# A pre-norm decoder layer: first normalisation split by batch, and the first projections reordered around it

## The reference

```python
x = x + attention(layernorm(x))          # 16 heads of 16, causal, Wq Wk Wv Wo with biases
x = x + cross_attention(layernorm(x), ctx, mask)   # 512 memory tokens, no weights
x = x + moe(layernorm(x))                # router, top 4 of 16 experts, gated FFN

def layernorm(x): return (x - mean(x)) / sqrt(var(x) + 1e-5)
Q = (X @ Wq.T + bq) * scale;  K = (X @ Wk.T + bk) * scale;  V = X @ Wv.T + bv
```

## Time and profile before

| | value |
|---|---|
| median of three runs | 232.58 us |
| the profiled execution's own time | 232.66 us |
| its span in the trace | 230.9 us |
| PE busy | 222.6 us, 96% |
| DVE busy | 179.4 us, 78% |
| ACT busy | 130.1 us, 56% |
| POOL busy | 75.2 us, 33% |

### The profile page before, as it was taken

How to read it: one execution, slowest core, us unless ns; L and a number is a source line. 1 busy time by engine, 2 the same in 40 slices (tenths; PEclk the granted TensorE clock), 3 DMA queues, 4 the chain that set the end, 5 groups by cost and what they waited for, 6 DMA issues and landing times.

```text
span 230.9 us, 4563 instructions
## 1 busy us (share of the span) xinstructions
PE 222.6 (96%) x1481; PEld 177.8 (77%) x1481; DVE 179.4 (78%) x431; ACT 130.1 (56%) x258; POOL 75.2 (33%) x65
## 2 busy tenths in 40 slices
PE   7999989998999999989999999999999999999995
PEld 2588767875485788778888888888888888888884
DVE  3779896969267458679889879879879879879775
ACT  2138999766341617384484384385385385375561
POOL 6621460001002010426426426425425435435222
PEclk9999999999999999999999999999999999999999
DMA  5991042000000000022422431331331330410002
GB/s 170 381 387 34 0 140 91 3 4 0 0 3 0 0 0 4 0 62 76 139 60 77 136 71 65 136 79 57 136 88 48 136 102 34 136 45 0 1 3 91
DMA packets 7856, 17.30 MB, mean 75 GB/s; under 512 B 913, under 2 KB 2978, under 8 KB 7714
## 3 DMA queue, kind: packets, MB, share of 16 engines
q1 hardware_dynamic: 7232, 16.52, 21.8%
q10 hardware_dynamic: 610, 0.60, 0.9%
HBM read 16.59 MB, written 0.52 MB: 74 GB/s over the span
## 4 chain that ended last, share of the span: by engine, by line
PE 79%; DVE 9%; ACT 6%; issue 3%; POOL 2%; POOLq 0%; DVEq 0%; ACTq 0%
PE PS L1119 34%; PE PS L1135 20%; PE PS L987 3%; ACT pr L382 3%; PE PS L1001 3%; PE PS L1085 3%; DVE masked L668 2%; PE PS L947 2%; PE PS L961 2%; PE PS L978 2%; PE PS L895 2%; PE PS L883 1%; DVE HL L798 1%; PE PS L1165 1%; DVE qpar L574 1%
## 5 line engine op out<-in xcount | busy, mean ns | idle before, releaser
L296 POOL TENSOR_TENSOR WLg<-raw_g,WHg 128x1024 fp32r<-128x1024 f32 x16 | 38.2, 2390 | 58.4 <-ACT WHg L352 58.4
L793 DVE SCALAR_TENSOR_TENSOR pt<-pt 128x512 f32<-128x512 f32 x30 | 49.4, 1646 | 4.2 <-DVE pt L789 2.2
L478 ACT ACTIVATE HH<-pt 128x512 fp32r<-128x512 f32 x30 | 18.9, 632 | 52.3 <-DVE pt L793 52.1
L1119 PE MATMUL PS<-XH,WHg 128*128 128x512 f32 x120 | 47.0, 392 | 0.0
L1119 PE MATMUL PS<-XL,WHg 128*128 128x512 f32 x120 | 46.9, 390 | 0.0
L1119 PE MATMUL PS<-XH,WLg 128*128 128x512 f32 x120 | 46.7, 389 | 0.0
L1135 PE MATMUL PS<-WHd,HH 128*128 128x256 f32 x120 | 35.3, 294 | 1.0 <-DVE HL L798 0.8
L1135 PE MATMUL PS<-WLd,HH 128*128 128x256 f32 x120 | 33.9, 282 | 0.0
L1135 PE MATMUL PS<-WHd,HL 128*128 128x256 f32 x120 | 33.9, 282 | 0.0
L303 POOL TENSOR_TENSOR WLd<-raw_w,WHd 128x512 fp32r<-128x512 f32 x16 | 20.7, 1296 | 32.9 <-ACT WHd L358 32.9
L798 DVE TENSOR_TENSOR HL<-pt,HH 128x512 fp32r<-128x512 f32 x30 | 22.2, 738 | 11.0 <-ACT HH L478 11.0
(11 more groups left out here) (154 smaller groups left out, 358.5 us busy)
## 6 DMA issues: line engine op xcount, KB each, us to landing
raw_g<-we_d SPq DMA_DIRECT2D x16, 512.0 KB, 4.0
raw_w<-we_d SPq DMA_DIRECT2D x16, 256.0 KB, 2.6
ctxT<-ctxT_d SPq DMA_DIRECT2D x1, 1024.0 KB, 10.1
ctx_sb<-ctx_d SPq DMA_DIRECT2D x1, 1024.0 KB, 12.3
wqkv<-wqkv_d SPq DMA_DIRECT2D x3, 256.0 KB, 6.1
out_d<-x SPq DMA_DIRECT2D x4, 128.0 KB, 1.7
rows<-rows_d ACTq DMA_DIRECT2D x1, 264.0 KB, 5.7
x<-x_d ACTq DMA_DIRECT2D x2, 128.0 KB, 2.8
```

The lines of the kernel that those rows point to most:

```text
L296: g.tensor_tensor(WLg[slot][:, :, :, :].rearrange("p k g f -> p (k g f)"), raw_g[slot][:, :], WHg[slot][:, :, :, :].rearrange("p k g f -> ...
L478: a.activation(HH[slot][:, m, :], hid[:, m, :], ACT.Copy).then_inc(hh_done, 1)
L793: v_.scalar_tensor_tensor(out=hid[:, m, :], in0=glu[:, m, :], scalar=GLU_MAX, in1=upc[:, m, :], op0=ALU.min, op1=ALU.mult).then_inc(hid_do ...
L1119: i = t.matmul(PS[:, 2 * m + part, :], w[slot][:, k, part, m * P:(m + 1) * P], xx[:, k, :], start=(n == 0), stop=(n == 3 * KD - 1))
```

## The change

The first normalisation is done for each batch by itself. On DVE: statistics of chunks 0 and 1 and their variances, then statistics of chunks 2 and 3, then xn of batch 0, variances of batch 1, xn of batch 1. POOL takes two powers over two columns in place of one over four, and sets the constant part of vp after them. PE turns batch 0, projects K and Q of the first half of the heads for batch 0, then turns batch 1, then projects K and Q for batch 1. ACT issues `rows` after `params` and the mask.

```diff
-            g.memset(vp[:, :, :, DH:HP], 1.0)
...
-                chunks = slice(0, NC) if n == 0 else slice((n - 1) % B * QC, (n - 1) % B * QC + QC)
+                chunks = slice(n % B * QC, n % B * QC + QC)
...
             rstds(0)
+            rstds(1)
+            g.memset(vp[:, :, :, DH:HP], 1.0)
...
-            act.dma_start(rows[:, :], rows_d.rearrange("(a n) -> a n", a=1).to_broadcast([P, 2 * D + E])).then_inc(row_in, 16)
             act.dma_start(params[:, :], params_d).then_inc(param_in, 16)
             act.dma_start(mask8[:, :], mask_d.rearrange("(a n) -> a n", a=1)).then_inc(mask_in, 16)
+            act.dma_start(rows[:, :], rows_d.rearrange("(a n) -> a n", a=1).to_broadcast([P, 2 * D + E])).then_inc(row_in, 16)
...
-            for c in range(NC):
-                dve.wait_ge(x_in[c], 16)
-                row_stats(x, c)
-            variances(0, range(NC))
-            normalise(x, 0, range(NC))
+            def first_stats(b):
+
+                for c in range(b * QC, (b + 1) * QC):
+                    dve.wait_ge(x_in[c], 16)
+                    row_stats(x, c)
+
+            first_stats(0)
+            variances(0, (0, 1))
+            first_stats(1)
+            normalise(x, 0, (0, 1))
+            variances(1, (2, 3))
+            normalise(x, 1, (2, 3))
...
-            for b in range(B):
-                transposes(xn, b, b, xn_done, (b + 1) * QC)
+            def project_half(j, m, bank, b):
+
+                pe.wait_ge(xT_done[b], 1)
+                for k in range(KD):
+                    i = t.matmul(PS[:, bank, b * S:(b + 1) * S], wqkv[:, j, k, m * P:(m + 1) * P], xT[:, k, b * S:(b + 1) * S],
+                                 start=(k == 0), stop=(k == KD - 1))
+                return i
...
+            transposes(xn, 0, 0, xn_done, QC)
             pe.wait_ge(qkv_in[1], 16)
-            project_heads(1, 0, 4, k_ps)
+            project_half(1, 0, 4, 0)
             pe.wait_ge(qkv_in[0], 16)
-            project_heads(0, 0, Q_BANK[0], q_ps)
+            project_half(0, 0, Q_BANK[0], 0)
+            transposes(xn, 1, 1, xn_done, NC)
+            project_half(1, 0, 4, 1).then_inc(k_ps, 1)
+            project_half(0, 0, Q_BANK[0], 1).then_inc(q_ps, 1)
             project_heads(1, 1, 5, k_ps)
```

More of the change, by code:

```diff
@@ L315, in _ @@
             low_gate_up(1, 1)
-            for n in range(1, 5):
+            for n in range(2, 6):
                 rstds(n)
@@ L540, in variances @@
             def variances(n, chunks):
-                dve.wait_ge(bn_done, NC if n == 0 else NC + n * QC)
+                dve.wait_ge(bn_done, (n + 1) * QC)
                 for c in chunks:
@@ L632, in context_scale @@
                 cs = slice(b * QC, (b + 1) * QC)
-                dve.wait_ge(rstd_done, b + 2)
+                dve.wait_ge(rstd_done, b + 3)
                 link(v_.tensor_scalar(xscale[:, cs], rstd[:, cs], D ** -0.5, None, ALU.mult))
@@ L725, in _ @@
             context_stats(1)
-            variances(3, (0, 1))
-            normalise(x3, 3, (0, 1))
+            variances(4, (0, 1))
+            normalise(x3, 4, (0, 1))
             context_max(2)
@@ L742, in _ @@
             context_stats(3)
-            variances(4, (2, 3))
-            normalise(x3, 4, (2, 3))
+            variances(5, (2, 3))
+            normalise(x3, 5, (2, 3))
             low_x(2, slice(S, S + P))
@@ L886, in _ @@
             pe.wait_ge(ident_done, 1)
-            for b in range(B):
-                transposes(xn, b, b, xn_done, (b + 1) * QC)
-            def project_heads(j, m, bank, done):
[L892 to L897, removed]
+            def project_half(j, m, bank, b):
[4 more added lines that the diff above has]
+                return i
+            def project_heads(j, m, bank, done):
+                project_half(j, m, bank, 0)
+                project_half(j, m, bank, 1).then_inc(done, 1)
+            transposes(xn, 0, 0, xn_done, QC)
             pe.wait_ge(qkv_in[1], 16)
-            project_heads(1, 0, 4, k_ps)
+            project_half(1, 0, 4, 0)
             pe.wait_ge(qkv_in[0], 16)
-            project_heads(0, 0, Q_BANK[0], q_ps)
+            project_half(0, 0, Q_BANK[0], 0)
+            transposes(xn, 1, 1, xn_done, NC)
+            project_half(1, 0, 4, 1).then_inc(k_ps, 1)
+            project_half(0, 0, Q_BANK[0], 1).then_inc(q_ps, 1)
             project_heads(1, 1, 5, k_ps)
```

## The result

The changed kernel takes 233.81 us (median of 16 runs, 233.07 to 235.06) against 232.80 us (16 runs, 232.44 to 234.33) for the kernel before: ratio 1.0036, 95% interval 1.0020 to 1.0052. It is slower, by 0.5 to 1.2 us; the prediction said 233.5, in a range of 232.6 to 234.2, and gave "slower" 0.80. The profiled execution has a span of 231.5 us, 0.6 more than before.

The account below looks back on a forecast made before the run. PE's completion of Q was taken to bound the kernel, shifting the end one for one: projections start 0.41 us earlier, but batch 1's transposes and copy lie bare, so 12.59 becomes 13.52, +0.93, giving 233.5 us, range 232.6 to 234.2.

Parts of the forecast that it names:

- The warm-up term: PE at the head: batch 0's transposes start when the 14 warm-ups end, 6.90; uncertain by up to +0.17 us.
- a sign of being wrong: DVE after the projections: queries starting before 13.1, against 13.5 expected, would show the forecast wrong.
- The weights term: Transfers of K's and Q's weights: Q's land at 8.3 for a use at 9.2, so zero.
- The rows' move: Transfer of rows, issued 1.0 us later: landing at 8.5, or 9.5 at the far end; taken as zero.
- The memset: POOL, vp's constant part, 0.94 us: may hold batch 1's xn to 9.3, but costs nothing by itself.
- The port: Rival, DVE against POOL: late rows let xb block bup and maskf, DVE is the end; +1.4, 234.0; chance 0.12.
- The clock: Rival, PE: longer gaps undo the clock's rise, half of 5 us lost; +0.93 + 2.5, 236.0; chance 0.04.
- Absorption of Q's shift: Rival, attention loop from 17 us on: it absorbs the shift; 0 to -0.2, 232.5; chance 0.12.
- The kept start: Rival, PE: gaps half as long, so the 0.41 us earlier start is kept; +0.3, 232.9; chance 0.08.

Follow-up runs that it names:

- e2: Kernel before with PE's new order alone; normalisation, memset and rows as before: ratio 1.0067 to the kernel before.
- e3: Changed kernel with batch 1's transposes between K and Q of batch 0: ratio 1.0003 to the kernel before.
- e9: e3 with vp's memset back ahead of the powers: ratio 0.9983 to the kernel before, median 232.38 us.
- e11: e1 (changed kernel, old order on PE) with vp's memset ahead of the powers: ratio 0.9987 to the kernel before.
- e1: Changed kernel with PE's old order put back; split normalisation, later memset and later rows stay: ratio 1.0021 to the kernel before.
- e6: Changed kernel with 12 warm-up matmuls instead of 14: ratio 1.0031 to the kernel before.
- e4: Changed kernel with rows issued ahead of params and the mask, as before: ratio 1.0064 to the kernel before.
- e5: Changed kernel with DVE's parity, bup and maskf ahead of its copy of xT: ratio 1.0040 to the kernel before.
- e10: Changed kernel with Q's weights issued on ACT's queue instead of SP's: ratio 1.0032 to the kernel before.
- e12: Changed kernel with five edits together, e9's two plus those of e5, e10 and e6: ratio 0.9992 to the kernel before.
- e7: Kernel before with 12 warm-up matmuls instead of 14: ratio 1.0008.
- e8: Kernel before with rows issued behind params and the mask, nothing else: ratio 0.9985.

## Why the prediction was right

| step | predicted | measured |
|---|---|---|
| transposes of batch 0, start | 6.90 | 6.34 |
| their copy on ACT | 7.60 | 7.05 |
| K of batch 0 | 8.36 | 7.79 |
| transposes of batch 1 | 10.04 | 9.69 |
| DVE's copy | 10.74 | 10.33 |
| PE's next load | 11.49 | 11.07 |
| Q complete | 13.52 | 13.08 |
| queries start | 13.5 | 13.11 |
| shift of the masked scores | +0.93 | +0.49 |
| time | +0.93 | +1.01 by medians, +0.84 by the ratio, 0.5 to 1.2 |

**What bounds.** Q's completion sets the end one for one: shown by the thirteen profiles of the table. The order on PE as the cause is shown from three sides: alone it costs 1.0 to 2.1 us (e2); with the transposes moved ahead by four records the loss is gone (e3, and clear of the noise with the memset early, e9); and put back, with the memset early, it leaves none (e11). Put back by itself it leaves half a microsecond, which is the memset's (e1 against e11).

**Where PE's gaps fall.** From batch 0's copy on, each length but one came as worked out (predicted in brackets): copy to K 0.74 (0.76), transposes to DVE's copy 0.64 (0.70), copy to next load 0.74 (0.75), load to Q complete 2.01 (2.03). The one is K to batch 1's transposes, 1.90 (1.68), which holds the wait for Q's weights.

**The warm-up term** was mis-sized. I read its end from one profile as a fixed 6.90, with 0.17 as its spread. In the eight profiles with the split normalisation and 14 warm-ups, the transposes of batch 0 start between 6.05 and 6.91, since the 14 took from 4.60 to 5.67 us, depending on when TensorE went over to its upper level. In the kernel before this is hidden behind xn; in the changed kernel it is the first link of the chain. In its profile it gave 0.56 us, the weights took 0.23 back, and 0.11 was gained in hand-overs: Q complete 0.44 ahead of the forecast. The queries, at 13.11, stand only just outside what the prediction named as a sign of being wrong (before 13.1). The shift over 16 runs, +0.84 by the ratio, lies nearer to the forecast of +0.93 than the profile's +0.50.

**The weights term** was wrong. "the later rows leave them more room, so zero too, with Q's 0.9 us as margin" rested on one landing, 6.1 us after the issue, in an execution in which these transfers came early: ten of the other eleven profiles with Q's weights on SP show more, up to 7.2. Q's weights landed at 8.72 here, 9.23 in e6, 9.33 in e4, against a use at 8.5 to 8.6, and PE stood for 0.23 to 0.75. The rows' move, which I took at zero, is worth about 0.65 us (e4, size loose). Without that move the change would have cost 1.5 us (1.0 to 2.0), which is the upper edge of the range that I gave. So the step that failed inside a forecast that fits is that of the rows and weights. That the total still fitted is in part luck: the warm-up ended 0.56 earlier than I took it to, while the weights cost 0.23 that I had not counted.

**The memset** cost nothing, as predicted, though it held xn for 0.6 us. The Trainium skill, SBUF — State Buffer (Who interferes with whom), says that a VectorE instruction in a two-port mode and a GpSimd one exclude each other, and that the one which is issued first gets the way. The traces agree: xn took 1.32 us beside the memset and 0.73 without it (e11). maskf at 1.22 beside xb in e9, and bup at 0.19 in the changed kernel, where xb took 3.32 and not 2.90, fit it too (read so, not tested).

**The rivals.** The port: its condition came true, rows landed at 9.8 (2.80 + 7.0), but bup took 0.19 and kT waited 0.41 us for PE; with e5, DVE's queue as the end is ruled out. The clock did not fall in the gaps: 16 loads behind the idle 1.02 us take 3.32, one every 0.21, and e10's behind 1.73 us also. The Trainium skill, TensorE: Matmul & The Clock Gate (HAM oscillation), describes a clock that falls behind longer waits between bursts than these, so no run here tests it. Absorption of Q's shift is ruled out by the spans. The kept start needed shorter gaps, and they came as worked out: from batch 1's transposes to the next load 1.38 us, against 1.45.

**Open.** The changed kernel's times spread from 233.07 to 235.06, those of the kernel before mostly within 0.45. The longest, 235.06, is the one with a mean granted clock of 0.985 (last section); the other fifteen end at 234.15. The landing of Q's weights and the end of the warm-up vary by 1.0 and 0.9 us, and both now lie on the path; no run separates their shares.

## What to carry to other kernels

When work is split so that it can start earlier, ask what the engine in the middle does between the halves: a transpose and its copy out need other matmuls beside them. Four records of cover brought the idle time from 1.02 to 0.32 us here. Before pulling an instruction forward, list everything that it waits for with its spread over several executions, transfers above all; a margin of 0.9 us against a landing seen once was none. A gap that is closed in one place opens at the next releaser, so change one thing at a time: five plausible edits together (e12) did no better than two (e9).

## What the runs showed of the hardware

- The landing of Q's weights, 256 KB issued by SP at the same 2.2 us, came 6.0 to 7.2 us later in twelve executions (8.2 to 9.4). With that transfer on a second queue, K's, on the first, landed 6.4 and 5.8 us after its issue (e10, e12), against 3.6 to 5.3 in eleven of the other twelve executions.
- TensorE ran at the lower of its two levels until some point between about 4 and 7 us, which differs from execution to execution: 14 identical warm-ups took 4.60 to 5.68 us (their steps were 0.43 us at the lower level and 0.21 at the upper), although the profile shows the full granted clock there. Where they stopped too early (e12), the four transposes behind them took 0.98 us, not 0.60.
- Idle times of 1.0 to 1.7 us between bursts in the head left the speed of the next matmuls as it was.
- A granted clock of 0.50 from about 101 to 104 us, behind a pause of TensorE of 0.8 us, appears in the profiles of the changed kernel and of e1 to e7, and not in those of before, e8, e9, e10 and e12, which have the same pause. It is a matter of the execution: the mean granted clock is 0.991 to 0.993 in some runs of one kernel and 1.000 in others. It costs 1.4 us where it falls and nothing at the end (the same 24 records, changed kernel and kernel before; start, length):

```profile
100.62 4.57 PE PS L1147 x24
```
```profile
100.13 3.14 PE PS L1135 x24
```

- Over the next experts the loss is made up. In the kernel before, PE's loads pause 0.28 to 0.47 us ahead of each expert's last group from 108.59 on; in the changed kernel the first such pause comes at 160.62 us:

```profile
108.59 0.19 PEld L1135 LDWEIGHTS PS<-WHd,HH 128*128 128x128 f32 x1 [0.28 <-DVE HL L798]
```
```profile
160.62 0.19 PEld L1147 LDWEIGHTS PS<-WHd,HH 128*128 128x128 f32 x1 [0.33 <-issue]
```

  Until then two experts take 16.68 us there instead of 17.1, and at 203 us the changed kernel is 0.55 us behind the kernel before again. Span minus queries' start is 218.27 to 218.43 with the low stretch and 218.32 to 218.45 without. So PE has slack in the expert stage, but the shift of Q finds none there; that it passes because the other engines start later as well is a reading, not tested.
- A lower mean granted clock, 0.985, goes with a longer time: in the runs of the kernel before beside e1 to e12, all nine with it took 233.92 to 234.20 us, against a median of 232.69 for the 31 with 1.000 and of 232.68 for the 49 with 0.991 to 0.993.
